# A second add on GpSimd in place of half of the column sums, in an attention stage

## The reference, cut to what matters

```python
t = _to_tokens(x)                      # 8 x 1024 x 384
t = t + _L1_attn_ref(_ln_t(t), ...)    # 12 heads of 32
...
scores = jnp.einsum('bhqd,bhkd->bhqk', q, k) * SCALE
probs = jax.nn.softmax(scores, axis=-1)
out = jnp.einsum('bhqk,bhkd->bhqd', probs, v)
```

## Time and profile before

| | us |
|---|---|
| median of 3 runs | 3006.07 (3001.13 to 3012.16) |
| profiled execution, its own time | 3010.64 |
| its span, first to last instruction | 3008.7 |
| TensorE busy | 2672.3 |
| VectorE busy | 1847.6 |
| ScalarE busy | 1586.1 |
| GpSimd busy | 1370.8 |
| mean granted TensorE clock | 0.949 |

### The profile page before, as it was taken

The page is one execution under the profiler, slowest core; times in us unless marked ns, Lnnn a source line. Parts: engine busy times, 40 slices in busy tenths (PEclk is TensorE's granted clock), DMA queues, the critical chain, the costliest instruction groups (busy, mean ns, idle before and its releaser), DMA issues. The chain is left out here.

```text
span 3008.7 us, 64263 instructions
## 1 busy us (share of the span) xinstructions
PE 2672.3 (89%) x23600; PEld 1302.3 (43%) x23600; DVE 1847.6 (61%) x2360; ACT 1586.1 (53%) x2582; POOL 1370.8 (46%) x1096
## 2 busy tenths in 40 slices
PE   4989756998997997998988988998859999999999
PEld 3555322453453453543543544543324444444444
DVE  6766246887777787887777778777433333333332
ACT  2323024666666665666666666666534444444443
POOL 2222034676676676676676677677620101111110
PEclk9989877999998998998999999999979999999999
DMA  4233232111211211212112112111020101101010
GB/s 149 87 115 106 79 97 83 51 30 30 93 30 48 74 35 60 61 36 83 39 36 83 41 30 71 42 30 43 1 105 22 43 25 38 42 21 42 21 42 21
DMA packets 68634, 164.41 MB, mean 55 GB/s; under 512 B 13569, under 2 KB 17470, under 8 KB 67326
## 3 DMA queue, kind: packets, MB, share of 16 engines
q1 hardware_dynamic: 68350, 160.60, 16.8%
HBM read 59.13 MB, written 37.75 MB: 32 GB/s over the span
## 5 line engine op out<-in xcount | busy, mean ns | idle before, releaser
L1356 POOL TENSOR_TENSOR b_pair<-b_ex 128x512 f32<-128x512 f32 x768 | 975.3, 1295 | 517.9 <-ACT b_ex L1232 516.5
L1232 ACT ACTIVATE b_ex<-b_st 128x512 f32<-128x512 f32 x1536 | 866.4, 596 | 485.2 <-PE b_st L903 464.2
L1066 DVE TENSOR_REDUCE b_mxp<-b_mx 128x4 f32<-128x2048 f32 x384 | 876.9, 2284 | 322.4 <-PE b_mx L919 309.6
L903 PE MATMUL b_st<-b_qst,b_kst 97*128 97x256 f16 (+1 forms) x3072 | 548.0, 282 | 117.5 <-ACT b_ex L1232 83.1
L903 PEld LDWEIGHTS b_st<-b_qst,b_kst 97*128 97x128 f16 (+1 forms) x3072 | 235.1, 99 | 452.1 <-ACT b_ex L1232 255.5
L1601 DVE TENSOR_TENSOR c_gs<-c_g,c_gs 128x512 f16<-128x512 f32 x192 | 132.7, 691 | 482.0 <-ACT c_gs L1674 482.0
L936 PE MATMUL b_pv<-b_ex,b_v 128*32 128x256 f32 x6144 | 422.8, 394 | 0.0
L1522 PE MATMUL c_hid<-c_z,c_wi 128*128 128x512 f16 x1728 | 405.3, 380 | 11.3 <-DVE c_z L1594 11.3
L1537 PE MATMUL c_acc<-c_gs,c_wo 128*128 128x512 f16 x1728 | 404.0, 379 | 0.4 <-DVE c_gs L1601 0.4
L1670 ACT ACTIVATE c_g<-c_hid,c_bias 128x512 f32<-128x512 f32 x192 | 131.4, 684 | 363.5 <-PE c_hid L1522 363.3
L1522 PEld LDWEIGHTS c_hid<-c_z,c_wi 128*128 128x128 f16 x1728 | 169.3, 98 | 227.5 <-issue 18.8
(11 more groups left out here) (162 smaller groups left out, 2754.1 us busy)
## 6 DMA issues: line engine op xcount, KB each, us to landing
a_x<-in_x SPq DMA_DIRECT2D x8, 1536.0 KB, 6.9
a_ob<-a_x SPq DMA_DIRECT2D x8, 1536.0 KB, 7.2
after_conv<-a_ob SPq DMA_DIRECT2D x24, 512.0 KB, 2.6
b_xl<-after_conv SPq DMA_DIRECT2D x8, 1536.0 KB, 6.9
b_qst<-b_staged0q SPq DMA_DIRECT2D x192, 64.0 KB, 2.0
b_kst<-b_staged0k SPq DMA_DIRECT2D x192, 64.0 KB, 2.0
b_v<-b_vstaged SPq DMA_DIRECT2D x24, 512.0 KB, 3.0
b_xr<-after_conv SPq DMA_DIRECT2D x8, 1536.0 KB, 6.6
```

The lines of the kernel that those rows point to most:

```text
L903: last = nc.tensor.matmul(st[n % NST][:, j * QUERIES:(j + 1) * QUERIES], kst[g][0:depth, s, kt * P:(kt + 1) * P], qst[g][0:depth, s, q0:q0 ...
L1066: nc.vector.reduce_max(mxp[x % 2][:, w // 2, :, w % 2], mx[:, :, :], AX_X).then_inc(mx_taken, 1)
L1232: nc.scalar.activation(ex[u % 2][e][s][:, :], st[n % NST][:, :], ACT.Exp, scale=SCALE).then_inc(exp_ready, 1)
L1356: nc.gpsimd.tensor_tensor(pair[u % 2][s][:, :], ex[u % 2][0][s][:, :], ex[u % 2][1][s][:, :], ALU.add).then_inc(pair_ready, 1)
```

## The change

In odd units, GpSimd adds the two 256-column parts of `pair[1][s]` once more, in place, into the first part (`fold_pair`), each one add behind the `add_pair` that it needs. TensorE leaves out the sums of an odd unit's first half and takes for its second half the folded part, behind a wait for the new semaphore `pair_folded`. A block so has three groups of sums instead of four, and the counts that `move_pv` and `add_pair` wait for follow.

```diff
@@ weigh (TensorE)
                 last.then_inc(pv_ready, 1)
-                pe.wait_ge(pair_ready, HG * (unit_no + 1))
+                if kh == 1 and e == 0:
+                    return
+                if kh == 1:
+                    pe.wait_ge(pair_folded, HG * (BLOCKS * b + x + 1))
+                else:
+                    pe.wait_ge(pair_ready, HG * (unit_no + 1))
+                at = e * QUERIES * (1 - kh)
                 for s in range(HG):
                     last = nc.tensor.matmul(pv[s * HEAD:(s + 1) * HEAD, QUERIES:BANK], ones[:, :],
-                                            pair[u % 2][s][:, e * QUERIES:(e + 1) * QUERIES],
+                                            pair[u % 2][s][:, at:at + QUERIES],
@@ move_pv (ScalarE)
-                act.wait_ge(sum_ready, 4 * block_no + 4)
+                act.wait_ge(sum_ready, 3 * block_no + 3)
@@ add_pair (GpSimd)
-                    pool.wait_ge(sum_ready, 2 * (unit_no - 2) + 2)
+                    pool.wait_ge(sum_ready, 3 * (BLOCKS * b + u // 2 - 1) + 2 + u % 2)
@@ new (GpSimd)
+            def fold_pair(b, u, s):
+                unit_no = IU * b + u
+                pool.wait_ge(pair_ready, HG * unit_no + s + 1)
+                nc.gpsimd.tensor_tensor(pair[1][s][:, 0:QUERIES], pair[1][s][:, 0:QUERIES],
+                                        pair[1][s][:, QUERIES:BANK], ALU.add).then_inc(pair_folded, 1)
@@ unit (GpSimd)
                     add_pair(b, u, s)
+                    if u % 2 and s:
+                        fold_pair(b, u, s - 1)
+                if u % 2:
+                    fold_pair(b, u, HG - 1)
                 if u < FIRST and out_proj:
                     add(b - 1, u)
```

More of the change, by code:

```diff
@@ L675, in attention_stage @@
         pv_ready = N.sem("pv_ready")
+        pair_folded = N.sem("pair_folded")
         sum_ready = N.sem("sum_ready")
```

## The result

The changed kernel takes 3134.46 us (median of 4 runs, 3134.01 to 3140.65), against 3003.6 us of the kernel before on the same chip: 1.044 times the time before, 95% interval 1.041 to 1.047, 131 us slower. The forecast was slower, 3051 us, with a range up to 3110. Sign and mechanism came as forecast, the size did not: the result lies 24 us above the range.

A forecast was written before the change was run, and what follows sets the result against it. It took TensorE to bound the plain stretch, busy 89% of the span. Terms 4 + 10 + 18 - 8 + 4 - 3 - 2 + 22 = +45 us gave 3051 us against the median 3006.07; range 2985 to 3110.

The forecast's parts named there:

- I take 0.63: Price in us of one GpSimd fold, start to start, read from `attended_low`; bounds 0.62 and 1.24; 242 us in all.
- the fourth scaling at 7.70: Plain blocks: VectorE's last `shift` scaling ends 7.70 us after T, the start of the odd unit's first GpSimd add.
- the multiply wants to start at 7.73: Plain blocks: VectorE's multiply is ready 7.73 us after the odd unit's first add starts, racing GpSimd's next add.
- rival 3: Queueing is worse: the multiply loses also in units 8 to 20, 35 blocks cost 1.3 us more; 3090 to 3120; chance 0.15.
- The estimate of 0.56 us: Alternative price of a 256-column fold from the skill's 4497 ns for 2048 elements; GpSimd's train would end 0.28 us earlier.
- Units 8, 10, 14, 16, 20: The multiply gets through before GpSimd's next add, but the delay eats the whole gain; 35 blocks, +4 us.
- Units 12 and 18: GpSimd's next add comes earlier; the multiply loses in 7 of 14 blocks, the wave 1.5 us later; +10 us.
- Clock: TensorE at 1.2 GHz behind stalls of 2 us or more, 1.7 us each in 6 + 7 blocks; +22 us.
- Last image: Units 8 to 18: GpSimd's next add comes first, the wave +3.0 us later in each of six blocks; +18 us.
- the other units, -2: The last image's units other than 8 to 18 were to gain 2 us in all.
- All other units: Units 6 and 22 -8 us, units 0 and 2 nothing, unit 4 +4, units 19 and 21 -3.
- All of it on the path: 53 us: TensorE's removed sums, 96 groups of 0.55 us in front of the even unit's second wave, if all counted.

The follow-up runs named there:

- experiment 5: Two variants of the changed kernel in which each head's fold has its own form and is timed apart; one execution each, 3130.71 and 3024 us.
- e3b_fold_224: The changed kernel with folds of 224 instead of 256 columns; 3070.14 us, ratio 1.022 to the kernel before.
- e1b_no_folds: The changed kernel without GpSimd's folds, keeping the leaner sums; 2966.18 us, ratio 0.988 to the kernel before.
- e2b_folds_only: The kernel before with all its sums, plus four folds into a spare tile, each waiting for the one before; 3070.02 us, ratio 1.022.
- e6_gap: The changed kernel with one more wait: each fold also waits for the fold before it; 3082.18 us, ratio 1.028 to the kernel before.
- e5_forms: The changed kernel with folds per head: in place, float16 output, second input from another tile, in place into the second half; 3130.71 us.
- e8_forms2: The changed kernel with folds per head: as is, float16 second input, 128 columns, 192 columns; 3024 us.

## Why the prediction was right in sign and wrong in size

**Right.** What is removed (768 records, 55 us busy), that `pair_folded` costs nothing, that the reduce keeps 2.28 us, that scalings and multiply lengthen behind GpSimd (528 and 1084 ns in the mean), that the wave's wait is where it shows, and that the granted clock falls. The Trainium skill (SBUF — State Buffer, "Who interferes with whom") says that whoever issues first holds the shared pair for its whole instruction. The multiply of unit 16, which stands 1.51 us behind an add that started 0.04 us sooner, agrees; that one scaling gets through at each boundary of GpSimd's train is what these timelines add.

**The step that failed: the price of the fold**, "I take 0.63". It was read from `attended_low`, whose second input is float16, which experiment 5 shows to be the shorter form (0.67 against 0.73). There was no float32 add of 256 columns in the trace of before, and I chose the near row rather than a price between it and the upper end. Four folds at 0.685 end the train at T+7.72 instead of T+7.47, "the fourth scaling at 7.70" became 7.95, "the multiply wants to start at 7.73" became 7.98, and the add comes at 7.87 to 7.94. The slack was 0.12 to 0.19 us, and 4 x 0.055 is 0.22. That is rival 3, which named the number ("the train ends 0.15 us later than I count", 3090 to 3120) and got 0.15 of the chances; the measured time lies above its range too, by the blocks listed below. I had not set the chance by the slack: a race decided by 0.15 us, with four terms each uncertain by some 0.05, is no better than even. And the price alone was not the whole gap: in e3b_fold_224, at 0.61 us a fold, the multiply still loses in units 8 and 20, since there the first scaling misses the fourth add, the other condition of rival 3. The estimate of 0.56 us from the Trainium skill's figure (GPSIMD Engine Reference, "Elementwise — side-by-side cycle accounting") was proportional; the line of experiment 5, extended to 2048 columns, gives 0.18 + 2048 x 0.0021 = 4.5 us, which agrees with its 4497 ns, but at 256 columns the fixed part is a quarter of the whole and the proportional estimate misses it.

**Term by term** (span, +123.5):
- Units 8, 10, 14, 16, 20: forecast +4 us, measured +41 (30 blocks at 1.30 or 1.45; in the five of the seventh image the race is won). The term that was mis-sized by the failed step.
- Units 12 and 18: forecast +10 (1.5 us in half of 14), measured +33 (2.53 in twelve, 1.21 in the two of the seventh image). The coin's toss fell the wrong way in all 14, and in twelve a loss cost more than I had counted: the fourth scaling too stood behind the add (it ends at T+9.02, the multiply at T+10.50 and not 9.4), one boundary more. Where the multiply alone lost, its price of 1.2 to 1.45 us was near the 1.3 to 1.5 that I had taken.
- Clock: +22 forecast, 13 blocks at 1.7 us. Measured are unit 13's +1.59 in six images, +10, and in the last image 1.6 to 1.9 us in each odd unit from 9 to 17 (9.1 to 9.4 us against 7.47) and 3.4 in unit 19, +13, which the last image's sum below holds too; near enough in sum, though by other blocks in part. Behind unit 18's wait, as long as unit 12's, nothing of the kind follows (unit 19 takes 7.85 us). The 30 plain blocks, whose waits are 1.66 and 1.81 us, show none of it (units 9, 11 and 17 keep their 7.85 and 7.78).
- Last image: forecast 18 - 2 + 10 of the clock = +26, measured +49. Its units 8 to 19 are near the forecast: +33 for 28, the multiply at T+10.4 and the wave at T+12.7 as counted. What I missed is units 0 to 7, +17 us: I put them under "the other units, -2", but they too have GpSimd's output adds right behind the folds, so that the race is lost there as well (in unit 2 the multiply ends at T+11.7). I read the timeline of one pair of that image and not of its first units.
- All other units: forecast -7, measured -11: -17 in the first six images, mostly unit 6 (12.21 to 10.21 us in the second to sixth) and units 0, 2, 19, 21 and 22, and +6 in the seventh. What makes the seventh longer there stays open.
- "All of it on the path: 53 us" for the sums: e1b_no_folds gives 34 for them, 0.43 us and not 0.55 in a plain unit. Why the rest of a group was hidden I did not try.

## What to carry to other kernels

Before adding work to an engine that has time to spare, look at who uses the memory that it shares, in the pauses that will be filled: here 281 us of "free" GpSimd work cost 168 us through five instructions of VectorE that had taken 1.2 us a block. Count boundaries, not time: each waiting instruction needs one of its own, so four tiny instructions in a row behind a long train cost more than one large one, and small copies that another engine can do belong there (ScalarE here). Where a forecast hangs on a race, work out its slack and the uncertainty of what precedes it, and let their ratio set the chance; and price a new instruction by a row of the same types, or by bounds.

## What the runs showed of the hardware that I had not expected

- Even an instruction on 8 partitions x 32 elements, 0.17 us alone, queues behind GpSimd: the four at unit 16 took 1.81 us, the second to the fourth 0.68 to 0.69 from start to start, paced by the folds.
- When GpSimd pauses for less than 0.1 us (0.07 to 0.08 between the last two folds of e2b_folds_only and e6_gap), two of VectorE's waiting instructions get in instead of one. A semaphore wait added on GpSimd made the kernel 52 us faster (e6_gap).
- GpSimd's small adds have a fixed part: 0.18 us + 2.1 ns per column fits the float32 adds from 128 to 512 columns; a float16 second input takes 0.06 us off at 256 columns, a float16 output or another tile takes off nothing (e5_forms, e8_forms2).
- TensorE's granted clock: behind the wait of 2.90 us in unit 12 the stretch that followed ran at 1.2 GHz in each of the first six images, behind that of 2.89 us in unit 18 in none of them. Behind the waits of 1.66 and 1.81 us of the changed kernel it never fell, but in e6_gap it fell behind nine of twelve waits of 1.74 to 1.76 us. So the length of the wait alone does not decide it in these runs, and what does stays open.
